# A head's first query tile: one 256-column score matmul instead of two of 128, with the low part added on VectorE

## The chip, the core and the metric

The program runs on one core of one Trainium2 chip. The metric is device time in microseconds (us) of one execution, as the median of the runs. Engine names are those of the profile: PE is TensorE's matmuls, PEld its weight loads, DVE is VectorE, ACT is ScalarE, POOL is GpSimd, SP is SyncE.

## What is computed

Four sequences of 512 tokens, width 1024, go through a layer norm, causal attention with 16 heads of 64 and rotary positions, a second norm with a residual, and then a low-rank mixture of experts with its own norm and residual. The change touches the scores alone:

```
q = rotary(h @ Wq); k = rotary(h @ Wk); v = h @ Wv      # (b, s, 16, 64)
logits = einsum('bhqd,bhkd->bhqk', q, k)
logits = where(causal, logits, -1e9) / sqrt(64)
out = einsum('bhqk,bhkd->bhqd', softmax(logits), v) @ Wo
```

All operands are float32. The kernel splits each into a high part in the matmul's reduced float32 type (F32R) and a low part, the rest, and adds up the products that matter.

## The kernel before

**Units and steps.** Two heads of one sequence make a unit; there are 32 (`UNITS`), numbered `u`. A unit has 8 steps `s` (`STEPS`). In each step TensorE computes an eighth of the q, k and v projections of unit u in three pieces (`project_third`), and between the pieces the attention of the unit before: the scores of one query tile of 128 rows (`scores`, one step behind), the transposes of the probabilities of an earlier tile (`turn_probs`, three steps behind), and in steps 0 and 4 the product with v (`attend`, for the unit before that). The 8 query tiles `q` of a unit are four of head 0 and four of head 1; tile `q` covers `128 * (q % 4 + 1)` key columns because of the causal mask. So q = 0 and q = 4 are the two first tiles, with 128 key columns each; there are 64 in the program, in steps 1 and 5 of a slot.

**Scores.** For a head, `q_hl` holds the high part of q on 64 partitions and its low part on the other 64, `k_hh` holds the high part of k on both halves of the partitions, and `k_lo` has the low part of k on one half and zeros on the other. Two matmuls with the same weights (`q_hl`) are added up in one bank of PSUM, `sc_ps[q % 2]`: against `k_hh` and against `k_lo` (helper `products`, line 1403).

**What follows a score tile.** Each engine runs its own instructions strictly in the order in which they are written; semaphores tie the engines together. For tile `g`:

1. VectorE, `negate` (line 1053): one operation adds the mask to the scores, scales by -SOFT, writes `prob` and the running minimum `nmax`; it waits for the scores (`s_done`).
2. ScalarE, `exponent` (line 740): exp with `nmax` as bias and the row sums.
3. VectorE, `invert` (line 1063): `rinv`, in the same step as `negate`.
4. GpSimd, `divide` (line 595): `prob` times `rinv`.
5. TensorE, two steps later, the transposes (line 1499); then ScalarE's copy `pT_hi` (line 751) and VectorE's `pT_lo` (line 1071).

Between these VectorE also makes, in fixed steps, the rotary products (line 1080, steps 3 and 6), the low part of q (`q_low`, line 1085, steps 4 and 5), of k with the copy to the other half (`k_low`, lines 1091 and 1092, steps 7 and 0), of v, and the sums `o_sum` (line 1105, steps 1 and 6). ScalarE's copy `o_low` (line 784) precedes the latter. GpSimd adds and subtracts pairs of weight columns into `w_sum` (lines 606 and 607) and makes the low parts of the weights (`w_lo`, line 613), on odd slots.

**How far TensorE may run ahead.** `scores` of tile g waits until `negate` of tile g-2 is done (`neg_done`), `turn_probs` waits for `prob_done`. Within these limits TensorE does not wait for the others.

**Two kinds of units.** In units 1 to 8 (called ahead units below) each unit also normalizes and transposes a tile of x for the second half of the program, with more work on VectorE (lines 990 to 1011 and 1042) and 8 more transposes on TensorE. Units 9 to 29 have none of it. After unit 31 TensorE goes on to the output projection and the experts. A unit's `negate` and `exponent` run one slot later than its projections; where this text says that VectorE is in unit u, its score tiles are meant. The GpSimd work on `w_sum` in step 5 falls beside the score tiles of even units, just after `divide` of q = 4.

Of the kernel before, what the change touches and what calls it, by code (L numbers as in the profile page):

```python
# [19 lines left out]
F32R = mybir.dt.float32r  # L20
ALU = mybir.AluOpType
# [3 lines left out]
P = 128  # L25
EMBED = 1024
SEQ = 512
# [6 lines left out]
QT = SEQ // P  # L34
# [33 lines left out]
def sandwich_kernel(nc, x, wqkv, wo, ar, bt, br, cos, sin, scratch, out):  # L68
    with ExitStack() as ctx:
        def sb(stack, name, shape, dt=F32):  # L70
            return stack.enter_context(nc.sbuf_tensor(name, shape, dt))

        def sem(name):
            return ctx.enter_context(nc.semaphore(name))
# [4 lines left out]
        sc_ps = bank[2:4]  # L79
# [54 lines left out]
        sB = ExitStack()  # L134
# [1 line left out]


        q_hl = sb(sB, "q_hl", [P, 2, 2, SEQ], F32R)
        k_hh = sb(sB, "k_hh", [P, 2, 2, SEQ], F32R)
        k_lo = sb(sB, "k_lo", [P, 2, 2, SEQ], F32R)  # L140
        w_sum = sb(sB, "w_sum", [P, EMBED])
        rope = sb(sB, "rope", [P, SEQ])
        rot = sb(sB, "rot", [P, SEQ])
        mask = sb(sB, "mask", [P, SEQ])
# [3 lines left out]
        prob = sb(sB, "prob", [P, 4, SEQ])  # L148
# [4 lines left out]
        rinv = sb(sB, "rinv", [P, 4])  # L153
        o_low = sb(sB, "o_low", [DH, SEQ])
        o_sum = sb(sB, "o_sum", [DH, 2, SEQ])

        hold_hi = xin[:, 1, :].rearrange("p (c t) -> p c t", c=KC)
        hold_lo = xn[:, 1, :].rearrange("p (c t) -> p c t", c=KC)
# [63 lines left out]
        qk_lo_done = sem("qk_lo_done")  # L222
        s_done = sem("s_done")
        neg_done = sem("neg_done")
        exp_done = sem("exp_done")
        inv_done = sem("inv_done")
        prob_done = sem("prob_done")
# [56 lines left out]
        gate_dve = sem("gate_dve")  # L284
# [5 lines left out]
        def late(count, first):  # L290

            return not isinstance(count, int) or count >= first

        def real(u):

            return not isinstance(u, int) or 0 <= u < UNITS

        def trailing(u, s, lag):


            at = s - lag
            a, q = u - 1 + at // STEPS, at % STEPS
            return a, q, STEPS * a + q
# [684 lines left out]
        def _(dve):  # L988
# [56 lines left out]
            def negate(u, s):  # L1045
                a, q, g = trailing(u, s, 1)
                if real(a):
                    n = P * (q % QT + 1)
                    dve.wait_ge(s_done, g + 1)
                    if late(g, 4):  # L1050
                        dve.wait_ge(t_done, g - 3)
                    dve.sem_inc(gate_dve, 1)
                    dve.tensor_tensor_reduce(prob[:, q % 4, 0:n], sc_ps[q % 2][:, 0:n], mask[:, SEQ - n:SEQ],  # L1053
                                             -SOFT, 3e38, ALU.add, ALU.min, nmax[:, q % 4:q % 4 + 1]
                                             ).then_inc(neg_done, 1)

# [67 lines left out]
            def slot(pair, b, half, ahead=False):  # L1124
                u = 2 * pair + b + UPH * half
                if isinstance(u, int) and u == 0:
                    first_slot()
                    return
                for s in range(STEPS):
                    negate(u, s)  # L1130
                    if prepares(u, ahead) and s == 4:
                        x_variance(ahead_tile(u) + 1)
# [266 lines left out]
        def _(pe):  # L1399
            def products(dst, terms, first, last):  # L1400

                for n, (lhsT, rhs) in enumerate(terms):
                    mm = pe.matmul(dst, lhsT, rhs, start=first and n == 0, stop=last and n == len(terms) - 1)  # L1403
                return mm
# [71 lines left out]
            def scores(u, s, b):  # L1476
                a, q, g = trailing(u, s, 1)
                if real(a):
                    ab = (b + 1 + (s - 1) // STEPS) % 2
                    i, h = q % QT, q // QT  # L1480
                    if q % QT == 0:
                        pe.wait_ge(qk_lo_done, 4 * a + 3 + h)
                        pe.wait_ge(qk_hi_done, 4 * a + 3 + h)
                    if late(g, 2):
                        pe.wait_ge(neg_done, g - 1)
                    qc, kc = slice(P * i, P * i + P), slice(0, P * i + P)
                    products(sc_ps[q % 2][:, kc], [(q_hl[:, ab, h, qc], k_hh[:, ab, h, kc]),
                                                   (q_hl[:, ab, h, qc], k_lo[:, ab, h, kc])], True, True
                             ).then_inc(s_done, 1)

            def turn_probs(u, s):
                a, q, g = trailing(u, s, 3)
# [56 lines left out]
            def slot(pair, b, half, ahead=False):  # L1549
                u = 2 * pair + b + UPH * half  # L1550
                n = pair + PAIRS * half
                for s in range(STEPS):
                    third = MM_STEP // 3

                    def project_third(k):
                        if real(u):
                            project(u, b, n, half, MM_STEP * s + third * k, third)

                    project_third(0)
                    if s == 2 and real(u - 1):  # L1560
                        v_turn(u - 1, x_count(u, half, ahead))
                    scores(u, s, b)
                    project_third(1)
                    turn_probs(u, s)
                    project_third(2)
                    if s == 0:
                        attend(u - 2, b, 0)
                    if s == (3 if isinstance(u, int) and u == UNITS + 1 else 4):
                        attend(u - 2, b, 1)
                    for c in x_chunks(u, s):  # L1570
                        x_chunk(1, c)
                    if ahead and s in HOLD_AT:
                        hold_chunk(u, HOLD_AT.index(s), half, ahead)

                    if isinstance(u, int) and STEPS * u + s in range(STEPS * UNITS, STEPS * UNITS + len(Y_FIRST)):
                        for k, c in Y_FIRST[STEPS * (u - UNITS) + s]:
                            y_half(0, 0, k, c, c + 1)
                    if isinstance(u, int) and u == UNITS + 1 and s < len(Y_SECOND):
                        for c in Y_SECOND[s]:
                            y_half(1, 1, 0, c, c + 1)  # L1580
# [180 lines left out]
```

## Time and profile before

| | |
|---|---|
| median of 3 runs | 1073.88 us |
| lowest and highest | 1073.83 and 1074.21 us |
| span of the profiled execution | 1072.2 us |
| PE busy | 1054.7 us, 98% |
| DVE busy | 754.3 us, 70% |
| ACT busy | 591.3 us, 55% |
| POOL busy | 439.6 us, 41% |
| granted TensorE clock, mean | 0.999 of 2.4 GHz |

The span goes from the first to the last instruction; the run's time has 1.7 us more around it. A busy share tells how much work an engine had. It doesn't tell whether the engine could have been late without anybody noticing, and this is what the waits and the order of time tell.

### The profile page before, as it was taken

How to read it: one execution, taken by the hardware profiler on the slowest of the kernel's cores; microseconds unless marked ns; L12 is line 12 of the kernel's file. 1: busy time of each engine (PE TensorE's matmuls, PEld its weight loads, DVE VectorE, ACT ScalarE, POOL GpSimd, SP SyncE). 2: the span in 40 equal slices, each digit the busy share in tenths (PEclk: the TensorE clock that was granted, in tenths of full speed). 3: DMA queues.
4: the chain of work that ended last, by engine and by line, in shares of the span. 5: the costliest groups of instructions: out<-in, count | busy, mean ns of one | idle time of the engine just before them, and what ended most of it. 6: DMA issues, size and time to landing. Idle time of an engine off the chain costs nothing.

```text
span 1072.2 us, 20069 instructions
## 1 busy us (share of the span) xinstructions
PE 1054.7 (98%) x5559; PEld 883.4 (82%) x5559; DVE 754.3 (70%) x2138; ACT 591.3 (55%) x1390; POOL 439.6 (41%) x422
## 2 busy tenths in 40 slices
PE   7999999999999999999999999999999999999996
PEld 6888888888878888888888888888888888888884
DVE  8777777776666666666666666666666877777777
ACT  7566666666555665565555656555576333334334
POOL 4153443435253635434352625344457322333221
PEclk9999999999999999999999999999999999999999
DMA  7022324242211256021111102010233223322311
GB/s 280 35 84 70 128 68 131 70 128 67 92 50 34 93 182 226 10 73 34 47 49 32 51 29 68 10 68 12 71 137 107 97 87 118 117 94 86 113 60 60
DMA packets 58663, 90.36 MB, mean 84 GB/s; under 512 B 3568, under 2 KB 36336, under 8 KB 58608
## 3 DMA queue, kind: packets, MB, share of 16 engines
q1 hardware_dynamic: 58464, 89.44, 25.3%
q8 instruction: 25, 0.41, 0.2%
q14 instruction: 30, 0.25, 0.1%
q10 hardware_dynamic: 144, 0.26, 0.1%
HBM read 64.52 MB, written 25.17 MB: 84 GB/s over the span
## 4 chain that ended last, share of the span: by engine, by line
PE 94%; DVE 2%; issue 1%; ACT 1%; POOL 0%; DVEq 0%; ACTq 0%; POOLq 0%
PE bank L1472 49%; PE bank L1403 32%; PE bank L1499 6%; PE bank L1631 2%; PE bank L1608 1%; PE bank L1445 1%; PE bank L1632 1%; PE bank L1433 1%; PE bank L1415 0%; DVE stats L1182 0%; ACT prob L740 0%; DVE k_hh L1092 0%; ACT k_hh L766 0%; PE bank L1659 0%; DVE big_lo L1034 0%
## 5 line engine op out<-in xcount | busy, mean ns | idle before, releaser
L1472 PE MATMUL bank<-big_hi,w_hi 128*128 128x512 f32 (+1 forms) x776 | 332.1, 428 | 0.3 <-DVE big_lo L1034 0.3
L595 POOL TENSOR_SCALAR prob<-prob,rinv 128x128 f32<-128x128 f32 (+3 forms) x256 | 150.0, 586 | 440.8 <-DVE rinv L1063 440.8
L740 ACT ACTIVATE prob<-prob,nmax 128x128 f32<-128x128 f32 (+3 forms) x256 | 144.0, 563 | 308.6 <-DVE nmax L1053 307.1
L1472 PE MATMUL bank<-big_hi,w_lo 128*128 128x512 f32 (+1 forms) x776 | 304.5, 392 | 0.0
L1472 PE MATMUL bank<-big_lo,w_hi 128*128 128x512 f32 (+1 forms) x776 | 302.3, 390 | 0.0
L1472 PEld LDWEIGHTS bank<-big_hi,w_lo 128*128 128x128 f32 x776 | 145.6, 188 | 33.0
L1071 DVE TENSOR_TENSOR pT_lo<-bank,pT_hi 128x128 fp32r<-128x128 f32 (+3 forms) x256 | 123.8, 483 | 55.9 <-ACT pT_hi L751 53.2
L1472 PEld LDWEIGHTS bank<-big_hi,w_hi 128*128 128x128 f32 x776 | 146.7, 189 | 16.6 <-issue 0.4
L1472 PEld LDWEIGHTS bank<-big_lo,w_hi 128*128 128x128 f32 x776 | 147.3, 190 | 11.7
L1053 DVE CUSTOM_DVE_ANT_0 prob<-bank,mask 128x128 f32<-128x128 f32 (+3 forms) x256 | 124.3, 485 | 17.5 <-PE bank L1403 13.7
L1063 DVE RECIPROCAL rinv<-rsum 128x1 f32<-128x1 f32 x256 | 40.8, 160 | 127.9 <-ACT prob L740 127.5
L1499 PE MATMUL bank<-ident,prob 128*128 128x128 f32 x640 | 111.8, 273 | 0.3 <-DVE pT_lo L1071 0.2
L751 ACT ACTIVATE pT_hi<-bank 128x128 fp32r<-128x128 f32 (+3 forms) x256 | 108.7, 425 | 2.2 <-PE bank L1499 0.7
L1499 PEld LDWEIGHTS bank<-ident,prob 128*128 128x128 f32 x640 | 83.1, 141 | 29.9 <-POOL prob L595 2.9
L674 POOL TENSOR_TENSOR res<-res,x 128x1024 f32<-128x1024 f32 x14 | 33.5, 2391 | 146.2 <-ACT res L705 146.2
L613 POOL TENSOR_TENSOR w_lo<-w_sum,w_hi 128x1024 fp32r<-128x1024 f32 x32 | 83.0, 2592 | 8.1 <-ACT w_hi L733 7.8
L1403 PE MATMUL bank<-k_lo,q_hl 128*128 128x128 f32 (+3 forms) x256 | 82.1, 321 | 0.0
L1403 PE MATMUL bank<-k_hh,q_hl 128*128 128x128 f32 (+3 forms) x256 | 80.6, 315 | 1.1 <-DVE k_hh L1092 1.1
L1403 PE MATMUL bank<-big_hi,w_hi 128*128 128x512 f32 x192 | 79.6, 415 | 0.0
L1403 PE MATMUL bank<-pT_hi,v_hl 128*128 128x512 f32 (+3 forms) x256 | 76.6, 311 | 0.0
L1403 PE MATMUL bank<-big_lo,w_hi 128*128 128x512 f32 x192 | 75.2, 392 | 0.0
L1403 PE MATMUL bank<-big_hi,w_lo 128*128 128x512 f32 x192 | 75.0, 391 | 0.0
(144 smaller groups left out, 1917.6 us busy)
## 6 DMA issues: line engine op xcount, KB each, us to landing
w_raw<-in_wqkv SPq DMA_DIRECT2D x48, 512.0 KB, 4.2
attention_out<-o_sum SPq DMA_DIRECT2D x64, 128.0 KB, 2.3
w_raw<-attention_out SPq DMA_DIRECT2D x16, 512.0 KB, 4.7
land<-in_x SPq DMA_DIRECT2D x16, 512.0 KB, 3.5
out<-res SPq DMA_DIRECT2D x14, 512.0 KB, 2.6
xin<-in_x SPq DMA_DIRECT2D x12, 512.0 KB, 5.7
xT_hold_hi<-xin SPq DMA_DIRECT2D x8, 512.0 KB, 3.6
xT_hold_lo<-xn SPq DMA_DIRECT2D x8, 512.0 KB, 5.4
```

The lines of the kernel that those rows point to most:

```text
L595: pool.tensor_scalar(p, p, rinv[:, q % 4:q % 4 + 1], 1.0, ALU.mult, ALU.mult).then_inc(prob_done, 1)
L613: pool.tensor_tensor(w_lo[:, m, :], src, w_hi[:, m, :].bitcast(F32), ALU.subtract).then_inc(w_lo_done[m], 1)
L674: pool.tensor_tensor(res[:, i, :], res[:, i, :], x1[:, i, :], ALU.add).then_inc(res_done, 1)
L740: act.activation(prob[:, q % 4, 0:n], prob[:, q % 4, 0:n], ACT.Exp, scale=-1.0, bias=nmax[:, q % 4:q % 4 + 1], accum_out=rsum[:, q % 4:q % ...
L751: act.activation(pT_hi[:, h, 0:i + 1, P * i:P * i + P], pt_ps[q % 2][:, 0:P * (i + 1)].rearrange("p (j t) -> p j t", j=i + 1), ACT.Copy).t ...
L1053: dve.tensor_tensor_reduce(prob[:, q % 4, 0:n], sc_ps[q % 2][:, 0:n], mask[:, SEQ - n:SEQ], -SOFT, 3e38, ALU.add, ALU.min, nmax[:, q % 4:q ...
L1063: dve.reciprocal(rinv[:, q % 4:q % 4 + 1], rsum[:, q % 4:q % 4 + 1]).then_inc(inv_done, 1)
L1071: dve.tensor_tensor(pT_lo[at], pt_ps[q % 2][:, 0:P * (i + 1)].rearrange("p (j t) -> p j t", j=i + 1), pT_hi[at].bitcast(F32), ALU.subtract ...
L1403: mm = pe.matmul(dst, lhsT, rhs, start=first and n == 0, stop=last and n == len(terms) - 1)
L1472: done = pe.matmul(grp_ps[(b + k) % 2][:, cols], w, xt[:, cols], start=at == 0, stop=at == GROUP_MM - 1)
L1499: last = pe.transpose(pt_ps[q % 2][:, P * j:P * j + P], prob[:, q % 4, P * j:P * j + P], ident[:, :])
L1631: pe.matmul(o_ps[:, 0:2 * ARW], x2T_hi[:, c, :], ar_hl[:, c, :], start=c == 0, stop=False)
```

## The change

`k_hh` and `k_lo` become the two halves of one tile `k_all`, so that a matmul can read the same 128 key columns of both through one operand. For the first tile of a head (q = 0 and q = 4) TensorE issues one matmul of 2 x 128 columns in place of two of 128 that were added up: the product with the high part lands in columns 0 to 127 of `sc_ps[0]`, that with the low part in columns 128 to 255. VectorE first adds the low product to the mask's diagonal block into a new tile `low_masked`, waits for its own result (semaphore `low_added`), and then does `negate` with `low_masked` in the place of the mask. The other six tiles of a unit stay as they were. No instruction changes its place against the others.

```diff
-        k_hh = sb(sB, "k_hh", [P, 2, 2, SEQ], F32R)
-        k_lo = sb(sB, "k_lo", [P, 2, 2, SEQ], F32R)
+        k_all = sb(sB, "k_all", [P, 2, 2, 2, SEQ], F32R)
+        k_hh, k_lo = k_all[:, 0, :, :, :], k_all[:, 1, :, :, :]
...
+        low_masked = sb(sB, "low_masked", [P, P])
...
+        low_added = sem("low_added")
...
                     dve.sem_inc(gate_dve, 1)
-                    dve.tensor_tensor_reduce(prob[:, q % 4, 0:n], sc_ps[q % 2][:, 0:n], mask[:, SEQ - n:SEQ],
+                    added = mask[:, SEQ - n:SEQ]
+                    if q % QT == 0:
+                        added = low_masked[:, :]
+                        dve.tensor_tensor(added, sc_ps[0][:, P:2 * P], mask[:, SEQ - P:SEQ], ALU.add).then_inc(low_added, 1)
+                        dve.wait_ge(low_added, 2 * a + q // QT + 1)
+                        dve.sem_inc(gate_dve, 1)
+                    dve.tensor_tensor_reduce(prob[:, q % 4, 0:n], sc_ps[q % 2][:, 0:n], added,
                                              -SOFT, 3e38, ALU.add, ALU.min, nmax[:, q % 4:q % 4 + 1]
                                              ).then_inc(neg_done, 1)
...
-                    products(sc_ps[q % 2][:, kc], [(q_hl[:, ab, h, qc], k_hh[:, ab, h, kc]),
-                                                   (q_hl[:, ab, h, qc], k_lo[:, ab, h, kc])], True, True
-                             ).then_inc(s_done, 1)
+                    if i == 0:
+                        pe.matmul(sc_ps[0][:, 0:2 * P].rearrange("p (a n) -> p a n", a=2), q_hl[:, ab, h, qc],
+                                  k_all[:, :, ab, h, kc], start=True, stop=True).then_inc(s_done, 1)
+                    else:
+                        products(sc_ps[q % 2][:, kc], [(q_hl[:, ab, h, qc], k_hh[:, ab, h, kc]),
+                                                       (q_hl[:, ab, h, qc], k_lo[:, ab, h, kc])], True, True
+                                 ).then_inc(s_done, 1)
```

## Rows read from the trace of the kernel before

**Rows 1.** The page: busy time of each engine, its share of the span, instructions.
```profile
PE 1054.7 (98%) x5559; PEld 883.4 (82%) x5559; DVE 754.3 (70%) x2138; ACT 591.3 (55%) x1390; POOL 439.6 (41%) x422
```
**Rows 2.** Timeline of PE (start, duration, both us): a first tile, then a second tile.
```profile
303.08 0.22 PE L1403 MATMUL bank<-k_hh,q_hl 128*128 128x128 f32 x1
...
303.53 0.40 PE L1472 MATMUL bank<-big_lo,w_hi 128*128 128x512 f32 x1
...
331.60 0.28 PE L1403 MATMUL bank<-k_lo,q_hl 128*128 128x256 f32 x1
...
331.96 0.39 PE L1472 MATMUL bank<-big_lo,w_hi 128*128 128x512 f32 x1
```
**Rows 3.** Waits of the whole run: who waited for whom, total us, times, longest.
```profile
ACT prob L740 <- DVE nmax L1053: 307.1, 203, 4.7
DVE rinv L1063 <- ACT prob L740: 127.5, 178, 1.9
DVE prob L1053 <- PE bank L1403: 13.7, 18, 2.3
DVE mv L996 <- DVE stats L1182: 3.2, 21, 0.2
PEld bank L1499 <- POOL prob L595: 2.9, 8, 0.6
```
**Rows 4.** Groups of DVE with shapes kept apart: total us, mean ns, idle before.
```profile
L1071 DVE TENSOR_TENSOR pT_lo<-bank,pT_hi 128x128 fp32r<-128x128 f32 x64 | 18.6, 290 | 0.0
```
**Rows 5.** Timelines of DVE and PE: the first tile of units 14, 15 and 16.
```profile
392.26 0.29 DVE L1053 CUSTOM_DVE_ANT_0 prob<-bank,mask 128x128 f32<-128x128 f32 x1
...
417.21 0.29 DVE L1053 CUSTOM_DVE_ANT_0 prob<-bank,mask 128x128 f32<-128x128 f32 x1
...
440.34 0.29 DVE L1053 CUSTOM_DVE_ANT_0 prob<-bank,mask 128x128 f32<-128x128 f32 x1
...
389.56 0.22 PE L1403 MATMUL bank<-k_hh,q_hl 128*128 128x128 f32 x1
...
438.30 0.22 PE L1403 MATMUL bank<-k_hh,q_hl 128*128 128x128 f32 x1
```
**Rows 6.** Waits from 487 to 755 us (units 18 to 28): total us, times, longest.
```profile
DVE prob L1053 <- PE bank L1403: 7.2, 12, 0.7
```
**Rows 7.** Timelines of DVE and PE: first tiles of ahead units 3 and 7.
```profile
118.41 0.29 DVE L1053 CUSTOM_DVE_ANT_0 prob<-bank,mask 128x128 f32<-128x128 f32 x1
118.62 0.08 DVE L1053 DVE_READ_ACCUMULATOR2_ANT nmax<- 128x1 f32 x1
...
219.64 0.29 DVE L1053 CUSTOM_DVE_ANT_0 prob<-bank,mask 128x128 f32<-128x128 f32 x1
...
215.84 0.22 PE L1403 MATMUL bank<-k_hh,q_hl 128*128 128x128 f32 x1
```
**Rows 8.** Timelines of DVE and POOL: after the second head's first tile, units 14, 16.
```profile
405.38 1.58 DVE L1085 TENSOR_TENSOR q_hl<-rot,q_hl 64x512 fp32r<-64x512 f32 x1
...
405.37 1.05 POOL L606 TENSOR_TENSOR w_sum<-w_raw 128x512 f32<-128x512 f32 x1
...
451.27 0.29 DVE L1053 CUSTOM_DVE_ANT_0 prob<-bank,mask 128x128 f32<-128x128 f32 x1 [0.43 <-PE bank L1403]
...
453.86 1.18 DVE L1085 TENSOR_TENSOR q_hl<-rot,q_hl 64x512 fp32r<-64x512 f32 x1
...
453.45 1.04 POOL L606 TENSOR_TENSOR w_sum<-w_raw 128x512 f32<-128x512 f32 x1
```
**Rows 9.** The same place in ahead unit 4, DVE and POOL.
```profile
157.88 0.97 DVE L1085 TENSOR_TENSOR q_hl<-rot,q_hl 64x512 fp32r<-64x512 f32 x1
...
157.26 1.04 POOL L606 TENSOR_TENSOR w_sum<-w_raw 128x512 f32<-128x512 f32 x1
158.26 1.49 POOL L607 TENSOR_TENSOR w_sum<-w_raw 128x512 f32<-128x512 f32 x1
```
**Rows 10.** Line 1092: shortest, median and longest duration in ns, first and last start.
```profile
L1092 DVE CAST k_hh<-k_hh x64: 420/424/2536, 38.5 to 803.2; 64x512 fp32r<-64x512 f32 x64
```

## The prediction

> **What bounds the kernel now.** I read the page first. TensorE is busy 98% of the span, VectorE 70%, ScalarE 55% [rows 1]. By this alone TensorE is the bound and VectorE has room for a small addition. The list of waits says otherwise. VectorE waited for the scores only 18 times before its 256 mask-and-minimum operations, 13.7 us in all, while ScalarE's exp waited for VectorE's `nmax` 203 times (307.1 us) and VectorE's reciprocal waited for that exp 178 times (127.5 us) [rows 3]. So in most steps the scores lie ready, and VectorE and ScalarE take turns: each waits for the other, and what one adds the other can't make up. VectorE's 30% of idle time lies inside this ring and is no reserve. A reserve is only the time in which VectorE waits for TensorE.
>
> So I compare how long the ring takes for two units (an even and an odd one) with how long TensorE takes. In the middle of the program the ring goes from 392.26 (unit 14) over 417.21 to 440.34 (unit 16): 24.95 and 23.13, together 48.08 us, without a wait for scores between. TensorE takes 438.30 - 389.56 = 48.74 us for the same two [rows 5]. The ring is only 0.66 us in 48.7 faster. VectorE's distance behind TensorE (start of its first tile behind the start of its scores) shrinks by as much, from 2.70 to 2.04 us.
>
> In the ahead units there is not even that. From unit 3 to unit 7 the ring takes 219.64 - 118.41 = 101.23 us, 50.6 for two units; at 219.64 it is 3.80 us behind TensorE [rows 7], and this is about as far as TensorE can get ahead: the weight loads of its transposes waited for GpSimd's `prob` 8 times, up to 0.6 us [rows 3]. There the ring sets the pace already.
>
> **What TensorE saves.** From the start of the first 128-column matmul to the second projection matmul behind the pair it is 303.53 - 303.08 = 0.45 us. A 256-column matmul with the same follower takes 331.96 - 331.60 = 0.36 us [rows 2]. So 0.09 us a tile, 64 tiles, 5.8 us, if TensorE were the bound. The new operand in two pieces of 128 columns has no row; I take it at the price of the plain one. If it cost as much as the pair, nothing would be saved. Two units of TensorE become 48.74 - 4 x 0.09 = 48.4 us.
>
> **What VectorE gets.** One add of 128 columns from PSUM: the like operation takes 0.29 us [rows 4]. Then it waits for its own result and a semaphore count before the old operation may start. The nearest row is bn_aggr behind bn_stats on the same engine, with the same wait and the same count in the code (line 996): 3.2 us in 21 times, 0.15 each, at most 0.2 [rows 3]. So each first tile is late by 0.29 + 0.15 = 0.44 us. The bounds: an operation without such a wait starts 0.21 us behind the start of one of 128 columns (118.41, 118.62) [rows 7]; with the longest wait it is 0.49. I take 0.44, because the code of that row is the same. Behind the waiting instruction on VectorE are the minimum, the reciprocal, `pT_lo` and all that follows; ScalarE's exp waits for it, GpSimd for the reciprocal. ScalarE as a rule stands idle at this point (203 of its 256 exps waited for `nmax` [rows 3]) and has nothing else to do meanwhile, so I let the whole 0.44 go through the ring. The name change from `k_hh` and `k_lo` to `k_all` costs nothing: the same operations on the same bytes.
>
> **Where 0.44 doesn't go through.** In even units, after q = 4, the next long operation is `q_low`. In unit 14 it began at 405.38, with GpSimd's w_sum at 405.37, and ended at 406.96; in unit 16 the tile had waited 0.43 us for TensorE, `q_low` began at 453.86, 0.41 us behind GpSimd's start at 453.45, and ended at 455.04 [rows 8]. Both ended 1.59 us behind GpSimd's start: the delay was swallowed, since VectorE was held up by GpSimd anyway and GpSimd starts when its weight work before that allows. So in even units only the first head's 0.44 counts. In the ahead units the same place looks worse: `q_low` starts 0.62 us behind GpSimd's first w_sum operation, and the second begins at 1.00 us [rows 9]. With 0.44 it comes at 1.06, just behind the start of the second. If it then has to wait for that one too (about 1.04 us alone, as the first), it ends at 1.00 + 1.04 + 0.69 = 2.7 us instead of 1.6: 1.1 us more, in units 2, 4 and 6.
>
> The Trainium skill (SBUF — State Buffer, "SBUF: two separate sides") says that GpSimd and a VectorE operation with two SBUF inputs share a pair of ports under an exclusive lock, and that whoever starts first keeps it for the whole instruction. The end times of rows 8 agree, and by that rule the 1.1 us of the ahead units come.
>
> **The sum**, in the ring's time, since the ring is the bound from unit 1 on. Two units of the middle: 48.08 + 0.44 (even) + 0.88 (odd) = 49.4 us, against 48.4 of TensorE: the ring is now the slower one by 1.0, VectorE falls back to the 3.8 us and TensorE waits. Then:
> - Ahead units 1 to 8: four odd ones 4 x 0.88 = 3.5; four even ones 4 x 0.44 = 1.8; 3 x 1.1 = 3.3. Together 8.6.
> - Units 9 to 29: eleven odd ones 9.7, ten even ones 4.4, together 14.1. From this go the waits for TensorE that the ring no longer has: 12 in six even units, 0.6 each [rows 6]. Those before q = 4 were swallowed before too, so half counts: 3.6. Left 10.5.
> - Unit 0 still waits for TensorE as before (the projections start there): 0. Units 30 and 31: four tiles, 1.8, of which ScalarE's own work for Wo may hide some: 1.2.
>
> Together 20.3 us on 1073.9: **1094 us** (span 1092.5). TensorE's 5.8 us buy nothing, they become waiting; the output stage after it is TensorE's and unchanged.
>
> **Rivals.** (1) TensorE stays the bound: the ring has more room than I read, for instance because TensorE's distance of up to 3.8 us is enough of a buffer. For it: 98% busy, hardly a wait of TensorE in the trace. Against it: the buffer is used once, while the shortfall of 1.0 us comes 15 times. It would give 1073.9 - 5.8 = 1068. Chance 0.06. (2) The wait for its own result costs nothing, 0.21 a tile: 4 x 0.42 + 4 x 0.21 = 2.5 in the ahead units (`q_low` then comes at 0.83, before the second GpSimd operation), 11 x 0.42 + 10 x 0.21 - 3.6 = 3.1 after, 0.6 at the end: 6.2, so 1080. The ring's two units would be 48.7, still above TensorE's 48.4. Chance 0.10. The Trainium skill (VectorE: DVE Perf Modes, "The DRAIN you can't avoid") says that a semaphore after each of a chain of copies cost nothing extra; by this the case would be this one, but the 0.15 us of rows 3 speak against it. (3) The copy on line 1092 loses its place to GpSimd's `w_lo`: it takes 0.42 us as a rule but once 2.54 [rows 10], and it starts close ahead of that work in every even unit. If the new phase tips it, ten even units lose 2.1 each: 1094 + 21 = 1115. Against it: in an even unit everything after `q_low` keeps its distances. Chance 0.05. (4) Gain and loss cancel, within 2 us of before: the pieces would have to meet by accident. 0.03. The forecast's own case has 0.76; in it the ends are 1086 (no 1.1 us in the ahead units, the one 2.5 us copy gone, short waits) and 1098.
>
> **How the numbers follow.** Cases: 1094 (0.76), 1080 (0.10), 1115 (0.05), 1068 (0.06), no change (0.03). The range 1080 to 1099 takes in the first two and leaves out 0.14 and some of their tails. A measurement of this kernel can tell about 0.2%, 2 us: slower 0.91, same 0.03, faster 0.06.
>
> **What would show it.** VectorE's waits for the scores (13.7 us before) almost gone after unit 0, TensorE's transposes waiting for `prob` in nearly every unit, 20 us or more in all, and TensorE's busy share down to 96%. The first tile's add and the old operation 0.44 us apart in start. Two middle units 49.4 us apart on both engines. `q_low` in units 2, 4 and 6 over 1.5 us. A first tile on TensorE 0.36 us from its start to the second matmul behind. Wrong, if two middle units take 48.4 us (TensorE's bound), or if the add and the minimum lie 0.2 us apart.

## The result and the profile after

The changed kernel takes 1095.33 us (median; 1095.17 to 1096.56), the kernel before 1073.97 us beside it (1073.83 to 1074.21). The ratio is 1.0199, with a 95% interval from 1.0187 to 1.0212. The span of the profiled execution went from 1072.2 to 1094.8 us, 22.6 us more. The profiled one is the slowest of the four (1096.56 us; the other three took 1095.17 to 1095.44), and 1.2 of its 22.6 us are no part of the median; they are found in units 30 and 31 below.

The page, first of before (the chain, which was not shown yet), then of after: busy time of the engines, and the shares of the chain that ended last.

```profile
PE 94%; DVE 2%; issue 1%; ACT 1%; POOL 0%; DVEq 0%; ACTq 0%; POOLq 0%
```
```profile
PE 1064.1 (97%) x5495; PEld 873.9 (80%) x5495; DVE 771.1 (70%) x2202; ACT 591.4 (54%) x1390; POOL 438.2 (40%) x422
...
PE 39%; DVE 20%; issue 20%; ACT 16%; DVEq 2%; POOL 1%; ACTq 1%; POOLq 0%
```

TensorE has 64 matmuls fewer than in [rows 1] and yet 9.4 us more of busy time, and it still reads 97% busy. Part of the waiting is counted as busy here: matmuls of 512 columns start some 0.23 us apart (399.54 and 399.77 below) and are each shown 0.39 to 0.40 us long, so a shorter stop between two of them leaves no gap. The chain says what the busy share hides: 94% of it lay on TensorE, now 39% does, and the rest goes round between VectorE, ScalarE and the issue of their instructions.

The waits of the whole run of after (who waited for whom: total us, times, longest):

```profile
ACT prob L742 <- DVE nmax L1061: 329.3, 197, 3.3
DVE rinv L1071 <- ACT prob L742: 128.5, 178, 2.1
...
PEld bank L1511 <- POOL prob L597: 25.8, 40, 2.2
...
DVE prob L1061 <- DVE low_masked L1058: 12.8, 64, 0.6
...
PE bank L1511 <- POOL prob L597: 9.2, 24, 1.7
...
DVE low_masked L1058 <- PE bank L1496: 3.2, 2, 2.2
...
DVE prob L1061 <- PE bank L1411: 2.1, 2, 1.3
```

VectorE's waits for scores fell from 13.7 us in 18 times to 5.3 us in 4. The weight loads of TensorE's transposes now wait 25.8 us for GpSimd's `prob`, against 2.9 us in [rows 3]. The 9.2 us of the transposes themselves fall within the same time and are not to be added. ScalarE's exp waits 22.2 us longer for `nmax`, nearly the whole loss: this is the addition, seen from ScalarE.

The new piece on VectorE (start, duration, both us; in brackets the idle time before), at the first tiles of units 14, 15 and 16:

```profile
403.24 0.29 DVE L1058 TENSOR_TENSOR low_masked<-bank,mask 128x128 f32<-128x128 f32 x1
403.73 0.29 DVE L1061 CUSTOM_DVE_ANT_0 prob<-bank,low_masked 128x128 f32<-128x128 f32 x1 [0.19 <-DVE low_masked L1058]
...
428.65 0.29 DVE L1058 TENSOR_TENSOR low_masked<-bank,mask 128x128 f32<-128x128 f32 x1
...
452.75 0.29 DVE L1058 TENSOR_TENSOR low_masked<-bank,mask 128x128 f32<-128x128 f32 x1
```

The old operation starts 0.49 us behind the addition. Two units take 452.75 - 403.24 = 49.51 us, where they took 48.08 [rows 5]. And TensorE at the same tiles, with a transpose between them:

```profile
399.41 0.29 PE L1496 MATMUL bank<-k_all,q_hl 128*128 128x256 f32 x1
399.54 0.40 PE L1480 MATMUL bank<-big_hi,w_hi 128*128 128x512 f32 x1
399.77 0.39 PE L1480 MATMUL bank<-big_lo,w_hi 128*128 128x512 f32 x1
...
406.59 0.33 PE L1511 MATMUL bank<-ident,prob 128*128 128x128 f32 x1 [0.24 <-POOL prob L597]
...
449.62 0.28 PE L1496 MATMUL bank<-k_all,q_hl 128*128 128x256 f32 x1
```

From the start of the new matmul to the second projection matmul behind it 0.36 us pass, as predicted, against 0.45 before. But VectorE is 3.83 us behind TensorE in unit 14 and 3.13 in unit 16 (2.70 and 2.04 before), and TensorE waits for `prob`. For this pair TensorE takes 449.62 - 399.41 = 50.21 us; in later pairs both engines take 49.7.

Where the 22.6 us came from is seen from VectorE's first tiles of units 1, 9 and 30 and its last operation on scores, first before, then after:

```profile
67.66 0.29 DVE L1053 CUSTOM_DVE_ANT_0 prob<-bank,mask 128x128 f32<-128x128 f32 x1
...
269.05 0.29 DVE L1053 CUSTOM_DVE_ANT_0 prob<-bank,mask 128x128 f32<-128x128 f32 x1
...
781.43 0.29 DVE L1053 CUSTOM_DVE_ANT_0 prob<-bank,mask 128x128 f32<-128x128 f32 x1
...
820.61 0.68 DVE L1053 CUSTOM_DVE_ANT_0 prob<-bank,mask 128x512 f32<-128x512 f32 x1
```
```profile
67.99 0.29 DVE L1058 TENSOR_TENSOR low_masked<-bank,mask 128x128 f32<-128x128 f32 x1
...
279.04 0.29 DVE L1058 TENSOR_TENSOR low_masked<-bank,mask 128x128 f32<-128x128 f32 x1
...
801.09 0.29 DVE L1058 TENSOR_TENSOR low_masked<-bank,mask 128x128 f32<-128x128 f32 x1
...
843.21 0.69 DVE L1061 CUSTOM_DVE_ANT_0 prob<-bank,mask 128x512 f32<-128x512 f32 x1
```

| stretch | before | after | more | predicted |
|---|---|---|---|---|
| up to unit 1 | 67.66 | 67.99 | 0.33 | 0 |
| units 1 to 8 | 201.39 | 211.05 | 9.66 | 8.6 |
| units 9 to 29 | 512.38 | 522.05 | 9.67 | 10.5 |
| units 30 and 31 (to that last operation) | 39.18 | 42.12 | 2.94 | 1.2 |
| output stage (to the end of the span) | 251.6 | 251.6 | 0.0 | 0 |

### The profile page after: what moved, and what is told of

It reads as the page before. It is cut to its first block, busy times and chain, and to the rows that moved or that the text cites. A ratio compares the mean times of both kernels' runs of the same rounds, so it can differ in the third digit from the quotient of the medians.

```text
span 1094.8 us, 20091 instructions
## 1 busy us (share of the span) xinstructions
PE 1064.1 (97%) x5495; PEld 873.9 (80%) x5495; DVE 771.1 (70%) x2202; ACT 591.4 (54%) x1390; POOL 438.2 (40%) x422
## 4 chain that ended last, share of the span: by engine, by line
PE 39%; DVE 20%; issue 20%; ACT 16%; DVEq 2%; POOL 1%; ACTq 1%; POOLq 0%
PE bank L1411 22%; PE bank L1480 11%; ACT prob L742 5%; DVE prob L1061 4%; DVE q_hl L1093 4%; ACT pT_hi L753 3%; ACT o_low L786 3%; DVE k_all L1100 2%; PE bank L1643 2%; PE bank L1511 2%; DVE low_masked L1058 2%; ACT k_all L768 1%; PE bank L1620 1%; ACT raw L772 1%; DVE pT_lo L1079 1%
## 5 line engine op out<-in xcount | busy, mean ns | idle before, releaser
L1480 PEld LDWEIGHTS bank<-big_lo,w_hi 128*128 128x128 f32 x776 | 147.2, 190 | 11.2
L1511 PEld LDWEIGHTS bank<-ident,prob 128*128 128x128 f32 x640 | 81.8, 141 | 52.3 <-POOL prob L597 25.8
L1061 DVE CUSTOM_DVE_ANT_0 prob<-bank,mask 128x256 f32<-128x256 f32 (+2 forms) x192 | 105.6, 550 | 4.6 <-PE bank L1411 2.1
L1411 PE MATMUL bank<-k_all,q_hl 128*128 128x256 f32 (+2 forms) x384 | 100.2, 342 | 0.0
L1411 PEld LDWEIGHTS bank<-k_all,q_hl 128*128 128x128 f32 x384 | 69.6, 188 | 13.7 <-DVE nmax L1061 0.3
```

What stands on the lines that cost most here:

```text
L1480: done = pe.matmul(grp_ps[(b + k) % 2][:, cols], w, xt[:, cols], start=at == 0, stop=at == GROUP_MM - 1)
L1511: last = pe.transpose(pt_ps[q % 2][:, P * j:P * j + P], prob[:, q % 4, P * j:P * j + P], ident[:, :])
```

## Experiments

All runs stand beside runs of the kernel before on the same chip (1074.15 to 1074.49 us). Each ratio is to that kernel, with its 95% interval. In the diffs `-` is the changed kernel, `+` the experiment, where nothing else is said.

**The two halves of the change apart.** First TensorE's half without the addition.

```diff
-                    if q % QT == 0:
-                        added = low_masked[:, :]
-                        dve.tensor_tensor(added, sc_ps[0][:, P:2 * P], mask[:, SEQ - P:SEQ], ALU.add).then_inc(low_added, 1)
-                        dve.wait_ge(low_added, 2 * a + q // QT + 1)
-                        dve.sem_inc(gate_dve, 1)
```

> TensorE's part alone: one 256-column matmul for each first tile, no add on VectorE (the low product of these 64 tiles is left out of the result). Theory (the ring of VectorE and ScalarE sets the pace where it is slower than TensorE): in the middle of the program the ring needs 48.1 us for two units and TensorE 48.4, so TensorE stays the bound and saves 0.09 us a tile, 0.37 us for two units; in ahead units 1 to 8 the ring needs 50.6 for two and was the bound before, so nothing is saved there. Together 1073.9 - 4.5 = 1069.5. Rival A (TensorE is the bound everywhere): 1068. Rival B (the operand in two pieces makes the matmul as dear as the pair): 1074, and 0.45 us from its start to the second matmul behind.

Measured: 1069.8 us (1069.53 to 1070.07), ratio 0.9958 [0.9941, 0.9974]. In the middle two units take TensorE 48.3 us in this run, and it is the bound; the ahead units take the ring 25.04 and 25.68 us as before, so there the saving is lost.

Then VectorE's half alone, with the two old matmuls; the addition's result goes unused.

```diff
-                        added = low_masked[:, :]
-                        dve.tensor_tensor(added, sc_ps[0][:, P:2 * P], mask[:, SEQ - P:SEQ], ALU.add).then_inc(low_added, 1)
+                        dve.tensor_tensor(low_masked[:, :], sc_ps[0][:, P:2 * P], mask[:, SEQ - P:SEQ], ALU.add).then_inc(low_added, 1)
...
-                    if i == 0:
-                        pe.matmul(sc_ps[0][:, 0:2 * P].rearrange("p (a n) -> p a n", a=2), q_hl[:, ab, h, qc],
-                                  k_all[:, :, ab, h, kc], start=True, stop=True).then_inc(s_done, 1)
-                    else:
-                        products(sc_ps[q % 2][:, kc], [(q_hl[:, ab, h, qc], k_hh[:, ab, h, kc]),
-                                                       (q_hl[:, ab, h, qc], k_lo[:, ab, h, kc])], True, True
-                                 ).then_inc(s_done, 1)
+                    products(sc_ps[q % 2][:, kc], [(q_hl[:, ab, h, qc], k_hh[:, ab, h, kc]),
+                                                   (q_hl[:, ab, h, qc], k_lo[:, ab, h, kc])], True, True
+                             ).then_inc(s_done, 1)
```

> VectorE's part alone: the two 128-column matmuls as before, VectorE makes the add (of stale columns into a tile that nobody uses) and waits for it, then the old operation with the mask as before; the result is that of before. Theory (ring): the ring is the bound with or without TensorE's saving, so the time is that of the changed kernel, 1094 to 1096, and TensorE waits about 6 us less. Rival A (TensorE is the bound and the loss comes from the new matmul's form): 1074 to 1076. Rival C (both engines' times add up): 1095 + 6 = 1101.

Measured: 1095.7 us (1095.21 to 1095.79), ratio 1.0198 [1.0181, 1.0215], the same as with the new matmul. The halves do not add up: the matmul alone gives 4.7 us, the addition alone costs 21.2, both together cost 21.4. With the addition in place, TensorE's saving is worth nothing that can be measured.

**The wait for its own result.** The addition stays, its result is not used, and the wait and the count behind it are gone.

```diff
-                        added = low_masked[:, :]
-                        dve.tensor_tensor(added, sc_ps[0][:, P:2 * P], mask[:, SEQ - P:SEQ], ALU.add).then_inc(low_added, 1)
-                        dve.wait_ge(low_added, 2 * a + q // QT + 1)
-                        dve.sem_inc(gate_dve, 1)
+                        dve.tensor_tensor(low_masked[:, :], sc_ps[0][:, P:2 * P], mask[:, SEQ - P:SEQ], ALU.add)
```

> The changed kernel, but VectorE doesn't wait for its add, and the old operation reads the mask (the low product of the first tiles is left out of the result). Theory (ring, 0.29 + 0.20 a tile of which the own wait and count are more than half): the step between the start of the add and that of the old operation falls from 0.49 to 0.21 us, so odd units cost 0.42 and even ones 0.21, q_low in units 2, 4 and 6 comes before GpSimd's second operation and stays near 0.8 us: 1074 + 6 = 1080. Rival D (the loss comes from the number of operations, not from the wait): 1094.

Measured: 1076.81 us (1076.67 to 1077.2), ratio 1.0023 [1.0013, 1.0033], 3 us below the expected 1080; unit 10 accounts for them (rival 2 below). The second head's first tile of unit 14 in VectorE's timeline of this run:

```profile
403.71 0.29 DVE L1057 TENSOR_TENSOR low_masked<-bank,mask 128x128 f32<-128x128 f32 x1
403.92 0.28 DVE L1058 CUSTOM_DVE_ANT_0 prob<-bank,mask 128x128 f32<-128x128 f32 x1
```

Without the wait the step is 0.21 us, with it 0.49. So 0.28 us a tile, 17.9 us over 64, are the wait and what it takes with it: without it the second operation begins 0.08 us before the first has ended. The whole run is 18.5 us faster. That the two figures are so close is in part chance: a late pair of units shrinks from 49.7 to 48.8 us, by less than four times 0.28, while in units 2, 4 and 6 the shorter step also avoids a meeting with GpSimd that costs about 1.1 us each (step by step below). Most of the loss comes from the wait, not from the addition itself. Which part the count has beside the wait wasn't tried.

**Which tiles pay.** The change on the first head's tile alone (q = 0), then on the second head's alone (q = 4). The diff is that of the first.

```diff
-                    if q % QT == 0:
+                    if q == 0:
...
-                        dve.wait_ge(low_added, 2 * a + q // QT + 1)
+                        dve.wait_ge(low_added, a + 1)
...
-                    if i == 0:
+                    if i == 0 and h == 0:
```

> The change for the first head of each unit alone (q = 0), the second head as before. Theory (every first head's 0.49 us goes through the ring): ahead units 8 x 0.49 = 3.9, units 9 to 29 21 x 0.49 = 10.3 less 3.6 for the waits for TensorE and perhaps 2.5 for the one long copy of unit 10, the end 1: 1083 to 1086. Two middle units 49.1 us. q_low of the second head in units 2, 4 and 6 as before, about 1.0 us. Rival (only the number of adds counts, half of the change costs half): 1085, but with two middle units at 48.9.

> The change for the second head of each unit alone (q = 4), the first head as before. Theory (in even units VectorE is held up by GpSimd at this place anyway, and in units 2, 4 and 6 the delay makes it meet GpSimd's second operation): ahead units 4 x 0.49 + 3 x 1.1 = 5.3; two middle units 48.1 + 0.49 = 48.6, where TensorE needs 48.6 too, so almost nothing there: 1079 to 1081. q_low in units 2, 4, 6 takes 1.57 us. Rival (nothing is swallowed: half of the change costs half, and the meetings with GpSimd on top): 1085 to 1087, two middle units 49.1 us.

Measured: 1082.93 us (1082.65 to 1083.22), ratio 1.0081 [1.0064, 1.0098], for q = 0 and 1079.34 us (1079.3 to 1080.95), ratio 1.0054 [1.0037, 1.007], for q = 4. The first is just below its 1083 to 1086, the second within its 1079 to 1081. VectorE's timeline with q = 4 alone, first tiles of units 14, 15 and 16:

```profile
395.84 0.29 DVE L1061 CUSTOM_DVE_ANT_0 prob<-bank,mask 128x128 f32<-128x128 f32 x1
...
420.76 0.29 DVE L1061 CUSTOM_DVE_ANT_0 prob<-bank,mask 128x128 f32<-128x128 f32 x1
...
444.36 0.29 DVE L1061 CUSTOM_DVE_ANT_0 prob<-bank,mask 128x128 f32<-128x128 f32 x1
```

The even unit takes 24.92 us, as long as unit 14 did before (24.95), the odd one 23.60 instead of 23.13 [rows 5]. This is the swallowed step of the prediction by itself: q = 4 costs nothing in even units and 0.47 in odd ones. The two runs alone cost 8.8 and 5.2 us, together 14.0, the full change 21.4. The traces show two causes for the gap of 7.4. The larger is unit 10: it took 27.86 us before, with one long copy and two waits for scores (step by step below), and takes 24.55, 24.41 and 24.92 us in the three runs. Each half earns this once, and so does the full change: 3.8 us of the gap. The other is the bound. Late pairs of units took 48.74 us before, TensorE's pace, where the ring alone takes less. They take 49.33 us with q = 0, 48.70 with q = 4 and 49.68 with both, so they cost 0.59, nothing and 0.94 us: the first growth of a pair is free in each of the two runs, but only once in the full change. Over units 9 to 29 without unit 10 the two halves together fall 2.6 us short of the full change.

**The addition one step earlier.** It was put into the gap in which VectorE waits for ScalarE's exp of the tile before, with its own wait for the scores; the wait for its result then finds it done.

```diff
-                        dve.tensor_tensor(added, sc_ps[0][:, P:2 * P], mask[:, SEQ - P:SEQ], ALU.add).then_inc(low_added, 1)
...
+            def add_low(u, s):
+                if s in (0, 4) and real(u - 1):
+                    dve.wait_ge(s_done, STEPS * (u - 1) + s + 1)
+                    dve.tensor_tensor(low_masked[:, :], sc_ps[0][:, P:2 * P], mask[:, SEQ - P:SEQ], ALU.add
+                                      ).then_inc(low_added, 1)
...
+                    add_low(u, s)
                     invert(u, s)
```

> The changed kernel with the add moved forward by one step: VectorE makes it in the step before, between the mask-and-minimum of the tile ahead and the reciprocal, where it waits for ScalarE's exp anyway (0.9 us as a rule); the wait for its own result is then long over. Theory (ring): the add costs the ring nothing in most units, TensorE is the bound in the middle again and its saving shows; in ahead units the second head's add costs 0.2 in a full step: 1070 to 1073. The new risk is that VectorE now waits for scores one step earlier, which holds while TensorE is more than about 2.3 us ahead; the ring then falls back until it is. Rival E (what counts is VectorE's busy time, wherever the add stands): 1094. Rival F (the earlier wait for scores keeps the ring behind, TensorE waits for it): 1078 or more.

Measured: 1080.47 us (1080.22 to 1080.62), ratio 1.0056 [1.0039, 1.0072]. My main expectation missed, its rival came. The wait that took the place of the one removed:

```profile
DVE low_masked L1068 <- PE bank L1503: 43.6, 35, 3.2
```

VectorE now stands at the addition for scores that TensorE has not made yet, and behind it stand the reciprocal and all that TensorE itself waits for. An operation put early in a strict order makes all that stand behind it wait for its inputs.

**Other work of VectorE into the gaps.** In the changed kernel `k_low` is written ahead of the reciprocal, where VectorE waits for ScalarE's exp; in a second kernel also `q_low` of the second head between the reciprocal and `pT_lo`, where it waits for ScalarE's `pT_hi`. Nothing is left out, and nothing is added. The diff is that of the second kernel; the first has the lines of `k_low` alone.

```diff
-                    leads = ahead or (isinstance(u, int) and u == UNITS - 1)
-                    if leads and s == 7:
+                    if s == 7 and real(u):
                         k_low(u, b, 0)
-                    if closing and s == 0 and real(u - 1):
+                    if s == 0 and real(u - 1):
                         k_low(u - 1, 1 - b, 1)
                     invert(u, s)
...
+                    if s == 5 and real(u):
+                        q_low(u, b, 1)
                     pt_low(u, s)
-                    if s == 0 and not closing and real(u - 1):
-                        k_low(u - 1, 1 - b, 1)
...
-                        if s in (4, 5):
-                            q_low(u, b, s - 4)
-                        if s == 7 and not leads:
-                            k_low(u, b, 0)
+                        if s == 4:
+                            q_low(u, b, 0)
```

> The changed kernel; VectorE makes both halves of k_low (lines 1091 and 1092, steps 7 and 0) ahead of the reciprocal, where it waits for ScalarE's exp, and not behind pT_lo. Theory (the ring's length counts, not VectorE's busy time, which is the same): the ring loses about 2 us in a unit of the middle and less than 1 in ahead units (where step 7 stands so already); TensorE is the bound in the middle with 48.4 for two units, the ahead units keep 2 us above it: 1071 to 1075. Rival E (VectorE's work counts wherever it stands): 1094. Rival F (the reciprocal comes later and TensorE waits for prob instead): 1080 or more.

> As the one before, and q_low of the second head (step 5) between the reciprocal and pT_lo, where VectorE waits for ScalarE's copy. Theory: ahead units too come down near TensorE's 25.0 us: 1068 to 1070, the time of TensorE's part alone or just below it. Rival (in even units q_low is now held up by GpSimd's w_lo, which started before it, for up to 2 us, and the ring gains nothing): 1073 to 1076.

Measured: 1072.43 us (1072.1 to 1072.59), ratio 0.9984 [0.9974, 0.9993], with `k_low` (TensorE takes 48.32 us for two units in the middle, but still 25.65 and 25.83 us for an ahead unit, where `q_low` meets GpSimd), and 1066.13 us (1065.78 to 1066.24), ratio 0.9925 [0.9908, 0.9941], with both: 29.2 us less than the changed kernel, 8.0 less than the one before on the same chip, and 2 us below what I expected. The place of `q_low` in the changed kernel, and then in this one (both unit 15):

```profile
441.00 0.17 DVE L1071 RECIPROCAL rinv<-rsum 128x1 f32<-128x1 f32 x1 [0.56 <-ACT prob L742]
442.14 0.56 DVE L1079 TENSOR_TENSOR pT_lo<-bank,pT_hi 128x384 fp32r<-128x384 f32 x1 [0.97 <-ACT pT_hi L753]
442.73 0.69 DVE L1093 TENSOR_TENSOR q_hl<-rot,q_hl 64x512 fp32r<-64x512 f32 x1
```
```profile
423.51 0.16 DVE L1071 RECIPROCAL rinv<-rsum 128x1 f32<-128x1 f32 x1 [0.56 <-ACT prob L742]
423.71 0.69 DVE L1093 TENSOR_TENSOR q_hl<-rot,q_hl 64x512 fp32r<-64x512 f32 x1
```

The 0.97 us of waiting now hold the 0.69 us of `q_low`, and the next score tile no longer stands behind it. The ahead units take TensorE 25.01 us, so the ring no longer holds it up there either.

**What is the change worth once the ring is short?** Three kernels have the same two reorderings, in the same lines: the kernel before; the kernel before with the addition added; and the new matmul without the addition.

> The kernel before with both reorderings of the run before (k_low of every unit ahead of the reciprocal, q_low of the second head between the reciprocal and the copy of pT_lo), without the changed matmul and without the addition. Theory A (the change's own worth is TensorE's, and the reorderings only make room for it): with the old matmuls TensorE sets every unit at its own pace, so the run loses only the waits of before that were VectorE's, 1071 to 1074 us, and the change plus reorderings (1066.1) is 5 to 6 us better than the reorderings alone. Rival B (the reorderings were the gain, the changed matmul is worth nothing): 1066 to 1068 us. Rival C (a reordering costs the old kernel, since its reciprocal comes 0.3 us later where nothing had to be cleared): 1075 us or more.

> The addition with its own wait on VectorE, the old matmuls, and both reorderings. Theory A (once VectorE's path between two tiles is shorter than TensorE's work, the addition costs nothing): the time of the reorderings alone, 1071 to 1074 us, 22 us less than the addition without the reorderings (1095.7). Rival D (the 0.49 us step is paid in part even then, by tiles whose scores come late): 1076 us or more.

> The changed matmul alone with both reorderings; the addition is left out, so the low product of the first tiles of both heads is left out of the scores. Theory A (TensorE bound in every unit, with or without the addition): 1065.5 to 1066.5 us, as with the addition (1066.1). Rival D (the addition still costs something): 1065 us or less; at 1063 it would cost 3 us.

| with both reorderings | old matmuls | new matmul |
|---|---|---|
| no addition | 1071.6 (0.9974 [0.9965, 0.9984]) | 1065.22 (0.9914 [0.9897, 0.993]) |
| addition and own wait | 1072.64 (0.9983 [0.9973, 0.9992]) | 1066.13 (0.9925 [0.9908, 0.9941]) |

The order as it was gives 1074.5 and 1069.8 in the upper row, 1095.7 and 1095.3 in the lower one. Now the halves add up: the matmul saves 6.4 and 6.5 us, the addition costs 1.0 and 0.9. (The lower right entry is the run above, on a chip where the kernel before takes 1074.15 us; on that of the other three it takes 1074.49, so 0.3 us of its differences may be the chip's.) Theory A holds in its main part; rival D keeps a small one: 1065.22 lies below theory A's 1065.5. TensorE's timeline at the first tiles of units 14 and 16, with both reorderings, first with the new matmul and the addition, then with the old matmuls:

```profile
385.24 0.28 PE L1493 MATMUL bank<-k_all,q_hl 128*128 128x256 f32 x1
...
433.56 0.28 PE L1493 MATMUL bank<-k_all,q_hl 128*128 128x256 f32 x1
```
```profile
387.80 0.22 PE L1400 MATMUL bank<-k_hh,q_hl 128*128 128x128 f32 x1
...
436.55 0.22 PE L1400 MATMUL bank<-k_hh,q_hl 128*128 128x128 f32 x1
```

These are 48.32 and 48.75 us for two units, so 0.11 a tile. VectorE's waits for scores of the same two runs:

```profile
DVE prob L1061 <- PE bank L1408: 33.9, 63, 1.3
DVE low_masked L1058 <- PE bank L1493: 20.7, 31, 2.2
```
```profile
DVE prob L1053 <- PE bank L1400: 83.9, 129, 2.3
```

This is the reserve that the kernel before lacked: 83.9 us in 129 times, against 13.7 in 18 [rows 3]. The addition is paid from it. With the new matmul, the addition leaves VectorE at its first tile of unit 30 at 772.26 instead of 772.22 us, and the last operation on scores begins 1.0 us later: what it still costs lies in units 30 and 31 alone.

## Why the prediction was right, step by step

- **The bound.** That VectorE and ScalarE's ring had only 0.66 us of room in two units, in spite of VectorE's 30% of idle time, was right and decided the sign. The middle pair was predicted at 49.4 us and took 49.51. That the idle time is no reserve holds for an operation that the ring waits for, as this addition ahead of `nmax`. For others it is one: with `k_low` and `q_low` of the second head moved into it, the changed kernel takes 29.2 us less with the same work on VectorE.
- **The step of a first tile, mis-sized.** I took 0.29 + 0.15 us; it is 0.29 + 0.20 (12.8 us in 64 waits). This is a term that the sum had too small, by 0.05 us in each first tile. The row I leaned on, `mv` behind `stats`, had the same wait and count but 0.15; the bound of 0.49 that I named was the true value. Why the two differ wasn't tried.
- **TensorE's saving.** 0.09 a tile was predicted; 0.11 was measured where TensorE is the bound, 6.4 us in all instead of 5.8. That it buys nothing in the change was right: with and without it the addition gives 1095.3 and 1095.7.
- **Ahead units, 8.6 predicted, 9.66 measured.** Four odd units cost 4.3 instead of 3.5 (the step, 0.98 a unit, and 1.4 in unit 7), the even ones 5.3 instead of 5.1. The meeting of `q_low` with GpSimd's second operation came as worked out. After, VectorE and GpSimd in unit 2:

```profile
109.49 1.57 DVE L1093 TENSOR_TENSOR q_hl<-rot,q_hl 64x512 fp32r<-64x512 f32 x1
```
```profile
108.46 1.04 POOL L608 TENSOR_TENSOR w_sum<-w_raw 128x512 f32<-128x512 f32 x1
109.46 1.04 POOL L609 TENSOR_TENSOR w_sum<-w_raw 128x512 f32<-128x512 f32 x1
```

`q_low` starts 0.03 us behind the second one and ends 2.60 us behind the start of the first (predicted 2.7, before 1.6): once GpSimd's operation has ended it takes 0.56 us more, not the 0.69 that I added. Without the own wait it starts ahead of it again, and `q_low` takes 0.76 us.
- **Units 9 to 29, 10.5 predicted, 9.67 measured**, by errors that offset each other. The odd units cost 11.2 instead of 9.7, and nine of the ten even ones 1.4 instead of 0.4. Against that stands unit 10, which went from 27.86 to 24.92 us, 3.4 less than with the 0.44 more that I gave it. It had one long copy of line 1092, which I had left in the main case and named only among its ends (and the wrong way in rival 3): it did not come again. The distance between the two tiles around it went from 6.30 to 4.05 us.

```profile
L1100 DVE CAST k_all<-k_all x64: 420/424/728, 38.6 to 823.8; 64x512 fp32r<-64x512 f32 x64
```

The longest copy is 728 ns now, 2536 before [rows 10]. Unit 10 also had two waits for scores, outside the stretch of [rows 6], and they are gone too. Before:

```profile
299.87 0.69 DVE L1053 CUSTOM_DVE_ANT_0 prob<-bank,mask 128x512 f32<-128x512 f32 x1 [0.32 <-PE bank L1403]
...
303.63 0.29 DVE L1053 CUSTOM_DVE_ANT_0 prob<-bank,mask 128x128 f32<-128x128 f32 x1 [0.78 <-PE bank L1403]
```

That these 3.4 us offset the rest was luck. The waits that late even units lost were sized nearly right: such a unit took 25.52 us with 1.2 us of them before and takes 25.50 now, where 0.44 - 0.6 would have made 25.36.
- **Units 30 and 31, 1.2 predicted, 2.94 measured.** Of the 2.94 some 1.2 go with TensorE's clock. TensorE had waited 1.71 us for `prob`; the windows of after show what came then (columns: window, its length, busy time and count of PE, PEld, DVE, ACT and POOL, granted clock, DMA share, GB/s):

```profile
818.00:820.50 2.50, 0.80 (x3) 0.30 (x2) 2.50 (x7) 2.42 (x6) 2.45 (x2) 1.00 0.05 13
820.50:823.00 2.50, 2.49 (x11) 2.36 (x12) 1.92 (x6) 1.62 (x4) 0.59 (x1) 0.61 0.92 274
822.00:824.20 2.20, 2.20 (x8) 1.92 (x8) 2.15 (x6) 1.23 (x4) 0.59 (x1) 0.50 0.92 313
```

The granted clock is 0.50 there, the lower of the two levels (1.2 GHz), and in the window from 818.00 to 820.50, with the wait, it was still 1.00. The addition alone has the same wait, 1.72 us, and kept 1.00:

```profile
822.00:824.20 2.20, 2.20 (x12) 1.81 (x12) 2.10 (x6) 1.34 (x4) 0.58 (x1) 1.00 1.03 406
```

From the first tile of unit 30 to the last operation on scores that run takes 1.16 us less. So the ring's own share is 1.8, nearly four steps of 0.49, with little hidden. The other three executions of the changed kernel left no trace. They are 1.1 to 1.4 us shorter, with a mean granted clock of 0.998 where the profiled one has 0.997. So the fall most likely belongs to this one execution and not to the kernel. Without it the change costs 21.4 us, as the medians have it, against the 20.3 that I had added up. Why the clock fell stays open.
- **Rival 2 (own wait free) at 1080** was the right next case, and its price was off: the run without the wait gave 1076.8. Its unit 10 takes 24.57 us, 3.3 less than before, and this is nearly the whole distance to 1080. (Its late even units of 25.19 us, where those of before took 25.52, were in the sum.) The Trainium skill (VectorE: DVE Perf Modes, "The DRAIN you can't avoid") reports a chain of copies that a semaphore after each did not lengthen. This case doesn't bear it out for an operation that waits on that semaphore: the wait cost 0.28 us from start to start, and the measurement decides.
- **Signs named ahead.** Seen: the transposes' waits of 20 us or more (25.8 of their loads), `q_low` over 1.5 us (1.57), 0.36 us at the new matmul. Not seen as named: these waits were to come in nearly every unit, but while VectorE is in unit 10, 12 or an even one from 16 to 28 there is none that the profile lists. The two middle units were to be 49.4 us apart on both engines, and on TensorE this pair takes 50.21. TensorE's busy share was to fall to 96% and fell to 97%.

## What to carry to other kernels

Ask of an idle time what it can take. Where two engines wait for each other, an operation put onto the path between them makes the path longer, however idle both look; here only the time in which VectorE waited for TensorE, or was held up by GpSimd anyway, could hide it. But the same idle time takes work that nobody in the ring waits for. Moving work onto such an engine pays only after its ring has been shortened: here the change lost 21 us, and saved 5.5 us against the same order without it once two of VectorE's steps, whose results are wanted only later, stood in its gaps. And the wait of one short operation for the one before it on the same engine can cost more than the operation: 0.28 us for the wait, 0.21 for the addition itself.

## What the runs showed of the hardware beyond the forecast

- VectorE waiting for its own result: start to start 0.49 us for 128 columns, against 0.21 us without the wait. With 64 of them gone the run was 18.5 us shorter, the meetings with GpSimd that they caused included.
- A VectorE operation of two SBUF operands (`q_low`) that starts 0.03 us behind a 1.04 us operation of GpSimd is held until that has ended: 1.57 us instead of 0.69.
- After a wait of 1.7 us TensorE's granted clock stayed at 1.00 in the profiled execution of one kernel and fell to 0.50 for a few us in that of another, which cost some 1.2 us.
